# Batched set-up of the decay constants after the first weight loads, and an output projection with four resident panels

## What is computed

```python
q = (x @ Wq).reshape(B, S, H, Dh);  v = (x @ Wv).reshape(B, S, H, Dh)
lam = sigmoid(beta)                              # one number per head, H = 16
def step(prev, vt):
    new = lam * prev + vt
    return (new, new)
states = scan(step, v)                           # along the sequence
y = (q * states).reshape(B, S, D)
y = layernorm(y) * ln_g + ln_b
y = (y * silu(x @ Wg)) @ Wo
x = layernorm(x + y)
gate, up = split(einsum('bsh,oh->bso', x, w_gate_up))
x = layernorm(x + einsum('bsi,hi->bsh', silu(gate) * up, w_down))
```

## Time and profile before

| what | us |
|---|---|
| runs shown | 2353.22 and 2458.63, median 2405.92 |
| profiled execution, device time | 2355.55 |
| its span on the slowest core (core 7) | 2353.9 |
| spans of the 8 cores | 2342.2 to 2353.9 |
| busy TensorE matmul / weight load | 1910.2 / 960.2 |
| busy VectorE / ScalarE / GpSimd | 580.5 / 373.7 / 111.1 |

### The profile page before, as it was taken

The page is one execution under the profiler, slowest core; times in us unless marked ns, Lnnn a source line. Parts: engine busy times, 40 slices in busy tenths (PEclk is TensorE's granted clock), DMA queues, the critical chain, the costliest instruction groups (busy, mean ns, idle before and its releaser), DMA issues.

```text
span 2353.9 us, 25536 instructions; the slowest of 8 cores (2342.2 to 2353.9 us)
## 1 busy us (share of the span) xinstructions
PE 1910.2 (81%) x9898; PEld 960.2 (41%) x9898; DVE 580.5 (25%) x1351; ACT 373.7 (16%) x424; POOL 111.1 (5%) x230
## 2 busy tenths in 40 slices
PE   2089899992189418999999999999999999997650
PEld 2034686430066214444444444444444444443220
DVE  3111223457821551101111111111111111111154
ACT  1500001530000022222121121112112112210002
POOL 0000000000000000001000000000000000000000
PEclk8599999995599758999999999999999999998875
DMA  5175133330023402435554254344435434422303
GB/s 72 23 127 101 20 71 61 72 66 36 0 47 63 125 18 43 83 72 89 90 90 72 54 99 80 67 76 84 78 54 91 85 62 86 75 51 36 57 16 143
DMA packets 32453, 161.04 MB, mean 68 GB/s; under 512 B 3668, under 2 KB 3668, under 8 KB 22100
## 3 DMA queue, kind: packets, MB, share of 16 engines
q0 software_dynamic: 29744, 142.62, 34.5%
q1 hardware_dynamic: 2596, 16.79, 1.9%
HBM read 293.62 MB, written 8.39 MB: 128 GB/s over the span
## 4 chain that ended last, share of the span: by engine, by line
PE 78%; DVE 10%; DMA 7%; issue 3%; ACT 2%; POOL 0%; DVEq 0%; ACTq 0%; POOLq 0%; SPq 0%
PE p L1132 19%; PE p L1038 19%; PE p L1069 18%; PE p L834 6%; PE p L494 5%; PE p L592 5%; PE p L372 4%; DMA warena<-wd_t 2%; DMA bbuf<-x_loc 2%; DMA warena<-wq 1%; DVE sqscr L790 1%; DVE sqscr L792 1%; DVE bbuf L799 1%; DVE sqscr L794 1%; DVE mscr L1187 1%
## 5 line engine op out<-in xcount | busy, mean ns | idle before, releaser
L1038 PE MATMUL p<-tbuf,warena 128*128 128x512 bf16 x2048 | 464.6, 380 | 2.0 <-DVE tbuf L977 1.7
L1069 PE MATMUL p<-tbuf,warena 128*128 128x512 bf16 x2048 | 462.9, 379 | 0.0
L1056 ACT ACT_TABLE_LOAD x128 | 164.2, 1283 | 1009.5 <-PE p L1038 1009.5
L1038 PEld LDWEIGHTS p<-tbuf,warena 128*128 128x128 bf16 x2048 | 200.6, 98 | 245.3 <-issue 5.1
L1069 PEld LDWEIGHTS p<-tbuf,warena 128*128 128x128 bf16 x2048 | 200.4, 98 | 241.6
L1132 PE MATMUL p<-warena,vbuf 128*128 128x512 bf16 x1024 | 231.3, 389 | 36.8 <-DMA warena<-wd_t 35.7
L1132 PE MATMUL p<-warena,qbuf 128*128 128x512 bf16 x1024 | 222.3, 379 | 0.0
L834 PE MATMUL p<-warena,bbuf 128*128 128x256 bf16 x1024 | 147.2, 277 | 86.9 <-DVE bbuf L799 43.6
L1148 DVE TENSOR_TENSOR bbuf<-bbuf,p 128x512 bf16<-128x512 bf16 x128 | 88.0, 687 | 399.6 <-PE p L1132 399.6
L372 PE MATMUL p<-tbuf,warena 128*128 128x512 bf16 x512 | 114.0, 386 | 79.7 <-DMA warena<-wq 79.7
L1132 PEld LDWEIGHTS p<-warena,vbuf 128*128 128x128 bf16 x1024 | 101.5, 100 | 166.0 <-issue 50.9
(11 more groups left out here) (125 smaller groups left out, 828.0 us busy)
## 6 DMA issues: line engine op xcount, KB each, us to landing
warena<-wgu_t POOLq DMA_DIRECT2D x128, 512.0 KB, 7.9
warena<-wd_t POOLq DMA_DIRECT2D x32, 1024.0 KB, 13.6
warena<-wq POOLq DMA_DIRECT2D x8, 1024.0 KB, 10.5
warena<-wv POOLq DMA_DIRECT2D x8, 1024.0 KB, 9.8
warena<-wg POOLq DMA_DIRECT2D x8, 1024.0 KB, 9.5
warena<-wo POOLq DMA_DIRECT2D x8, 1024.0 KB, 9.5
sscr<-x_loc SPq DMA_DIRECT2D x8, 1024.0 KB, 7.1
out_loc<-sscr SPq DMA_DIRECT2D x8, 1024.0 KB, 4.2
```

The source lines that it names most:

```text
L1038: inst = t.matmul(p[gbk][:, 0:NT], warena[:, (j % 2) * GUSL + k * OPW + ot * 128: (j % 2) * GUSL + k * OPW + (ot + 1) * 128], tbuf[:, k * ...
L1056: inst = sc.activation(sscr[:, SIL_OFF + (gg % 2) * NT: SIL_OFF + (gg % 2 + 1) * NT], p[gbk][:, 0:NT], AF.Silu)
L1069: inst = t.matmul(p[ubk][:, 0:NT], warena[:, (2 + j % 2) * GUSL + k * OPW + ot * 128: (2 + j % 2) * GUSL + k * OPW + (ot + 1) * 128], tbuf ...
```

## The change

Three things.

1. The GpSimd block with the first two Q panel loads and the `x_car` load moves from behind the decay constants to ahead of them. In the list of TensorE nothing moves; in the lists of VectorE and ScalarE the constants still stand between the transposes and the first Q eviction.
2. The constants are computed in batches: all 32 products into 4096 columns of `sscr`, then 16 masks, then 32 exponentials; then 8 iotas into 8 columns of `tscr`, 8 products, 8 exponentials, 8 products, with one wait between batches.
3. WO holds 4 panels, in slots 0 to 3. For each half of the panels the outer loop runs over the token chunks and the inner one over the 4 panels. The load of a panel of the second half waits for the last group that reads its slot in the first half (`wo_slot_free`). The residual of chunk `ci` waits for `attn_ci` of its own chunk instead of the end of WO; in the list of VectorE it still stands behind all evictions.

```diff
-    for h in range(H):
-        @blk.vector
-        def _(v, h=h):
-            v.wait_ge(sV, mil["llbc"] if h == 0 else cnt["V"])
-            v.wait_ge(sP, mil["ident"])
-            if h > 0:
-                v.wait_ge(sS, mil[("dexp", h - 1)])
-            tick(v.tensor_scalar_mul(sscr[:, 0:128], tscr[:, 0:128],
-                                     llbc[:, h:h + 1]), "V")
...
-    for st in range(NCH):
-        @blk.gpsimd
-        def _(g, st=st):
-            if st == 0:
-                g.wait_ge(sS, mil["decay_done"])
-            else:
-                g.wait_ge(sV, mil[("rmul", st - 1)])
...
+    @blk.vector
+    def _(v):
+        v.wait_ge(sV, mil["llbc"])
+        v.wait_ge(sP, mil["ident"])
+        for h in range(H):
+            v.tensor_scalar_mul(sscr[:, h * 128:(h + 1) * 128],
+                                tscr[:, 0:128], llbc[:, h:h + 1])
+            inst = v.tensor_scalar_mul(sscr[:, 2048 + h * 128:2048 + (h + 1) * 128],
+                                       tscr[:, 128:256], llbc[:, h:h + 1])
+        mil["dmul_all"] = tick(inst, "V")
+
+    @blk.gpsimd
+    def _(g):
+        g.wait_ge(sV, mil["dmul_all"])
+        for h in range(H):
+            inst = g.affine_select(sscr[:, h * 128:(h + 1) * 128],
...
+        mil["dmask_all"] = tick(inst, "P")
+
+    @blk.scalar
+    def _(sc):
+        sc.wait_ge(sP, mil["dmask_all"])
+        for h in range(H):
+            sc.activation(decay[:, h * 128:(h + 1) * 128],
+                          sscr[:, h * 128:(h + 1) * 128], AF.Exp)
...
+        mil["decay_done"] = tick(inst, "S")
+
+    @blk.gpsimd
+    def _(g):
+        g.wait_ge(sS, mil["decay_done"])
+        for st in range(NCH):
+            inst = g.iota(tscr[:, st:st + 1], [[1, 1]],
...
-    for pi in range(NPAN):
-        slot = 2 + pi % 2
+    PH = min(4, NPAN)
+    NHALF = NPAN // PH
+    for pl in range(PH):
         @blk.gpsimd
-        def _(g, pi=pi, slot=slot):
-            if pi >= 2:
-                g.wait_ge(sT, mil[("opdone", pi - 2)])
-            else:
+        def _(g, pl=pl):
+            if pl == 0:
                 g.wait_ge(sT, mil[("gpdone", NPAN - 1)])
-            mil[("wop", pi)] = panel_dma(g, "o", pi, slot)
+            mil[("wop", pl)] = panel_dma(g, "o", pl, pl)
+
+    for half in range(NHALF):
+        if half >= 1:
+            for pl in range(PH):
+                @blk.gpsimd
+                def _(g, half=half, pl=pl):
+                    g.wait_ge(sT, mil[("wo_slot_free", half - 1, pl)])
+                    mil[("wop", half * PH + pl)] = panel_dma(
+                        g, "o", half * PH + pl, pl)
         for ci in range(NCH):
+            n2c = ci // (NCH // NN2)
+            for pl in range(PH):
+                pi = half * PH + pl
+                bk = wo_banks[ogrp % 3]
...
+                    if ci == NCH - 1:
+                        mil[("wo_slot_free", half, pl)] = cnt["T"]
...
         def _(v, ci=ci, xsl=xsl, mc=mc):
             dwait(v, mil[("xld", ci)])
-            if ci == 0:
-                v.wait_ge(sV, mil["attn_done"])
+            v.wait_ge(sV, mil[("attn_ci", ci)])
```

More of the change, by code:

```diff
@@ L330, in build_program @@
-    mil["wred_done"] = cnt["V"]
     def panel_dma(g, which, pi, slot):
@@ new lines, in _ @@
+    @blk.gpsimd
[3 more added lines that the diff above has]
+            inst = g.affine_select(sscr[:, h * 128:(h + 1) * 128],
+                                   sscr[:, h * 128:(h + 1) * 128], [[1, 128]],
+                                   ALU.is_ge, -1e30, base=0,
+                                   channel_multiplier=-1)
+        mil["dmask_all"] = tick(inst, "P")
[5 more added lines that the diff above has]
+                          sscr[:, h * 128:(h + 1) * 128], AF.Exp)
+            inst = sc.activation(wpow[:, h * 128:(h + 1) * 128],
+                                 sscr[:, 2048 + h * 128:2048 + (h + 1) * 128],
+                                 AF.Exp)
+        mil["decay_done"] = tick(inst, "S")
@@ new lines, in _ @@
+    @blk.gpsimd
[3 more added lines that the diff above has]
+            inst = g.iota(tscr[:, st:st + 1], [[1, 1]],
+                          base=(TOK - 1) - st * 128, channel_multiplier=-1,
+                          allow_small_or_imprecise_dtypes=True)
+        mil["rcol_all"] = tick(inst, "P")
+    @blk.vector
+    def _(v):
+        v.wait_ge(sP, mil["rcol_all"])
+        for st in range(NCH):
+            inst = v.tensor_scalar_mul(sscr[:, st * H:(st + 1) * H],
+                                       llbc[:, 0:H], tscr[:, st:st + 1])
+        mil["rmul_all"] = tick(inst, "V")
@@ new lines, in _ @@
+    @blk.scalar
+    def _(sc):
+        sc.wait_ge(sV, mil["rmul_all"])
+        for st in range(NCH):
+            inst = sc.activation(sscr[:, 2048 + st * H:2048 + (st + 1) * H],
+                                 sscr[:, st * H:(st + 1) * H], AF.Exp)
+        mil["rexp_all"] = tick(inst, "S")
+    @blk.vector
+    def _(v):
+        v.wait_ge(sS, mil["rexp_all"])
+        for st in range(NCH):
+            inst = v.tensor_scalar_mul(wredT[:, st * H:(st + 1) * H],
+                                       sscr[:, 2048 + st * H:2048 + (st + 1) * H],
+                                       llbc[:, H:H + 1])
+        mil["wred_done"] = tick(inst, "V")
@@ L806, in build_program @@
         bank_r[b] = ("V", mil["y2_done"])
+    wo_banks = [4, 5, 6]
     ogrp = 0
-    wo_banks = [4, 5, 6]
-    for pi in range(NPAN):
-        slot = 2 + pi % 2
+    PH = min(4, NPAN)
+    NHALF = NPAN // PH
+    for pl in range(PH):
         @blk.gpsimd
-        def _(g, pi=pi, slot=slot):
-            if pi >= 2:
-                g.wait_ge(sT, mil[("opdone", pi - 2)])
-            else:
+        def _(g, pl=pl):
+            if pl == 0:
                 g.wait_ge(sT, mil[("gpdone", NPAN - 1)])
-            mil[("wop", pi)] = panel_dma(g, "o", pi, slot)
-        for ci in range(NCH):
-            bk = wo_banks[ogrp % 3]
-            @blk.tensor
-            def _(t, pi=pi, slot=slot, ci=ci, bk=bk, ogrp=ogrp):
-                if ci == 0:
[L827 to L853, removed]
@@ new lines, in _ @@
+            mil[("wop", pl)] = panel_dma(g, "o", pl, pl)
[7 more added lines that the diff above has]
+                        g, "o", half * PH + pl, pl)
+        for ci in range(NCH):
+            n2c = ci // (NCH // NN2)
+            for pl in range(PH):
+                pi = half * PH + pl
+                bk = wo_banks[ogrp % 3]
+                @blk.tensor
+                def _(t, half=half, ci=ci, pl=pl, pi=pi, bk=bk, n2c=n2c,
+                      ogrp=ogrp):
+                    if ci == 0:
+                        dwait(t, mil[("wop", pi)])
+                    wtb(t, bk)
+                    for k in range(KT):
+                        gk = (k // NDT) * NDT * NN2 + (k % NDT) * NN2 + n2c
+                        t.wait_ge(sV, mil[("y2", gk)])
+                        inst = t.matmul(
+                            p[bk][:, 0:PW],
+                            bbuf[:, k * TOK + ci * 128: k * TOK + (ci + 1) * 128],
+                            warena[:, pl * WSL + k * PW: pl * WSL + (k + 1) * PW],
+                            start=(k == 0), stop=(k == KT - 1))
+                    mil[("omm", ogrp)] = tick(inst, "T")
+                    bank_w[bk] = ("T", cnt["T"])
+                    if ci == NCH - 1:
+                        mil[("wo_slot_free", half, pl)] = cnt["T"]
+                @blk.vector
+                def _(v, ci=ci, pi=pi, bk=bk, ogrp=ogrp):
+                    v.wait_ge(sT, mil[("omm", ogrp)])
+                    v.wait_ge(sV, mil[("y2dt", ((ci + 1) * D - 1) // TOK)])
+                    tick(v.tensor_copy(
+                        qbuf[:, ci * D + pi * PW: ci * D + (pi + 1) * PW],
+                        p[bk][:, 0:PW]), "V")
+                    mil[("oev", ogrp)] = cnt["V"]
+                    bank_r[bk] = ("V", cnt["V"])
+                    if pi == NPAN - 1:
+                        mil[("attn_ci", ci)] = cnt["V"]
+                ogrp += 1
@@ L854, in build_program @@
+    mil[("opdone", NPAN - 1)] = cnt["T"]
     mil["attn_done"] = cnt["V"]
-    if c.stop == "WO":
-        return dbg_finish()
     for ci in range(NCH):
```

25 lines of the change are left out of this document (removed).

## The result

The changed kernel takes 2302.92 us (median), the kernel before 2357.58 us on the same chip: a ratio of 0.9781 with a 95% interval of 0.9769 to 0.9793, so 2.2% faster. Runs in which the cores of a die show a lower clock are left out of every ratio but not of the medians, which is why 2302.92 by 2357.58 would give 0.9768. The profiled execution has its slowest core at 2301.4 us (core 2), where before it was 2353.9 (core 7).

A forecast was written before the change was run, and what follows sets the result against it. TensorE was taken to bound the kernel nearly everywhere, so only its gaps ahead of the feed-forward could change. Sum: 2355.55 - 65.7 (head) + 16.7 (WO) = 2306.6, so 2307 us, range 2295 to 2322.

The forecast's parts named there:

- the line at 2%: Whole kernel: 2308.4 us, 2% faster, about what a measurement can tell; the forecast lay on it within its own bounds.
- The head: Stages up to Q's end: loads first and constants in batches end Q at 174.7 instead of 240.44, gain 65.7 us.
- the two bounds: Constants ahead of Q: products and exponentials not overlapped, gain 60.4 us; masks as dense as the products, gain 67.1.
- The cover of panel 2: In Q: panel 2 lands at 87, TensorE needs it at 91.8, so 5 us of cover and no wait.
- The refill: In WO: the second half's four panel loads take 28.4 us from first issue to last landing, loss 16.7 us.
- the fit cited from the Trainium skill: WO's loads: 2.0 us plus bytes at 436 GB/s per DMA; four panels 21.2 us, loss 9.5, time 2299; edge case.
- Costed at nothing: V, scan, G and the feed-forward keep their instructions, `attn_ci` frees nothing, and the first feed-forward loads stay covered: 0 us.
- Constants don't batch: Rival, head: a table load with every exponential, 48.6 us more, gain only 17.1, time 2355; chance 0.05.
- late loads: Rival, Q and WO: refill or `x_car` later than thought, head gain 60.4, WO loss 20.4, time 2316; chance 0.18.
- quicker refill: Rival, WO: the queue moves faster, 21 us for the four panels, loss 9.5, time 2299; chance 0.14.
- slower: Rival, WO: panels land one after another at 22.4 us each, loss 77, time 2367; chance 0.03.
- the chance of 0.52: Whole kernel: the probability given to faster by over 2%, against 0.46 for within 2% and 0.02 for slower.

The follow-up runs named there:

- e2: The kernel before with only WO changed as in the change; three runs count, 2364.93, 2366.38 and 2394.65 us, ratio 1.0122.
- e1: The changed kernel with WO put back as it was before (two slots, panels outside); 2292.39 us, ratio 0.9741.
- e10: The changed kernel with e8's head and WO reordered: chunks 0-3, then 4-7 on panels 0-3, then panels 4-7, no early evictions; lowest 2282.09 us, no ratio.
- e5: The changed kernel with the second half of WO going panel by panel, chunks inside; 2290.53 us, ratio 0.9708.
- e8: The changed kernel with the chunk batches behind later Q groups and x_car loaded in four parts; two lowest runs 2288.39 and 2288.53 us, no ratio.

## Why the prediction was right

It forecast 2307 in a range of 2295 to 2322; the time is 2302.92, and the ratio, 0.9781, lies just beyond the line at 2% on which the forecast stood.

- *The head.* Forecast 65.7 us, measured 67.6. Which wait follows which came out as written: panel lands, four groups, a gap that ends with an eviction, no wait for panel 2. Within it the terms were a little high: 16 masks took 3.95 us, not 4.6, the 8 short exponentials 0.95, not 1.8, and VectorE's batches of eight 1.20, not 1.4, so TensorE went on at 73.7 instead of 76.5, after a start 1 us late (49.5). One term was low: the 28 groups behind the gap took 99.1 us, not 98.2. That the instructions of a batch overlap, the choice between the two bounds, was right, and went further than I took it: eight 0.22 us exponentials in 0.95. The cover of panel 2, put at 5 us, was about 3.5: its load, issued at 68.20, took 18.4 us, and VectorE evicts the last group ahead of it at 90.1.
- *The refill.* Forecast 28.4 us from the first issue to the last landing, loss 16.7; measured 673.7 - 644.5 = 29.2, loss 15.4. The two differences go opposite ways: the last panel was 0.8 us later than thought, but behind it the 29 groups took 64.06 us where 64.6 + 1.2 for the low clock stood in the sum. Of the loss 13.5 are waits; the three groups between them took 3.1 to 3.3 us instead of 2.2, at a granted clock of 0.57 to 0.76. By the fit cited from the Trainium skill ("DMA: Bandwidth & Descriptors", "Anatomy of one DMA") the four would have taken 21 us, an estimate; with all eight cores loading, the trace has 29.2, and the measurement decides. No run has one core alone. e2 has the loss without the new head, and e1, with the head and WO as before, has none.
- *Costed at nothing.* V, scan and G came to +1.0 on the two slowest cores (+0.1 in the mean of eight), what lies behind WO to -1.3 (-0.7): within the spread between cores. `attn_ci` frees nothing, as forecast: from the end of WO to the first matmul of the feed-forward there are 103.6 us before and 103.3 after.
- *The rivals.* "Constants don't batch" is refuted by the two table loads, "late loads" and "quicker refill" by the two sizes above, "slower" by the 29.2 us, where it needed 77.

Head and refill both came out better than forecast, by 1.9 and 1.3 us, and that is most of the distance from 2306.6 to 2302.92. That the forecast was close to the 2% line was right too; which side the kernel fell on hung on such terms of 1 to 3 us, which the rows of before did not settle, and the chance of 0.52 says so. That side is luck.

## What to carry to other kernels

With hand-written lists, a load or an eviction stands where the source has it. Before batching a slow chain, look in each engine's list at what is queued behind it. Here it was the loads on GpSimd and the evictions on VectorE, two blocks apart from each other: moving the loads alone gained 31 us of Q's end and left a wait of 46.9 for the first eviction, batching alone gained 39 and left the loads late. Keeping more panels resident, in this order of the loops, moves the loads from "one per panel" to "all at a turn"; it pays only if the groups that it makes possible can also be evicted, and if the turn needs one panel and not all. And when an edit that should close a gap does nothing, see whether the gap's releaser has changed; that names the second cover.

## What was not expected of the hardware

The feed-forward, the same instructions in every kernel, took from its first to its last matmul 1367 to 1375 us on the eight cores of the kernel before, and 1379 on the slowest core of e1, where core 2 of the same execution took 1367. Of these 12 us, 7 are in the waits for `wd_t` (38.3 against 31.0); in its first 200 us the granted clock was 0.98 against 0.99; the rest stays open. In e10 it is 1381 on core 1. It is up to 10 us of the slowest core's time, nearly what e5 or e8 gained, so for edits of that size the stages of the trace were the better witness than the time.

Second, short instructions in one block overlap more than their durations say: 32 exponentials with 0.29 us each came 0.20 apart, eight short ones with 0.22 each took 0.95 together, and 16 masks took 3.95.
